# Gated cross-attention with sparse feed-forward on one core: attention in turns of four tiles of scores instead of two, with the loads spread out

## The chip, the cores and the metric

The kernel runs on one core of a Trainium2 chip. The time is the device time of one execution in microseconds (us), median over runs. TensorE (PE in the rows, PEld its weight loads), VectorE (DVE), ScalarE (ACT), GpSimd (POOL) and SyncE (SP, which only issues DMAs here) run in parallel; each works through its own list of instructions in order, and semaphores tie them together.

## The reference

`x` is 32 sequences of 64 tokens with 512 features. Attention has 32 heads of 128 over a context of the same shape, with a bias and a mask of keys; the feed-forward picks one row of 32 in each block by a low-rank score.

```python
x = x + tanh(g_xattn[0]) * xattn(layernorm(x), ctx, mask, bias, Wq, Wk, Wv, Wo)
x = x + tanh(g_ffn[0]) * ffn(layernorm(x), c1, c2, w1, w2t)
# xattn: q, k, v = h @ Wq, c @ Wk, c @ Wv   (32 heads x 128)
#        probs = softmax(q k^T / sqrt(128) + bias, masked); out = (probs v) @ Wo
# ffn:   idx = argmax in each block of 32 of (x @ c1.T @ c2.T)      (1792 = 56 blocks)
#        h = relu(w1[idx] . x);  out = h @ w2t[idx]
```

All of it is float32. The big products are made from high and low parts: three matmuls (hi hi, hi lo, lo hi) in place of one (`three`, L1438 to L1441).

## The kernel before

The kernel has three stages, one behind the other on TensorE.

1. Projections q, k, v of all tokens, in 94 units of seven products each, with results stored to HBM (0 to about 960 us).
2. Attention (about 947 to 1498 us). A *slot* is one tile of 128 tokens (two sequences, a "pair" in the code) with one group of 4 heads. An *iteration* is 8 slots, which share one loaded block of q, k, v (2 MB each), of bias (1 MB) and of Wo. 8 iterations (all head groups) make a half of the tokens; there are 16 iterations and 128 slots. Two slots are a *duo* (DUOS = 64), for which TensorE does: `scores` (q k^T, 64 small matmuls for two duos, L1506), `probs_t` (four transposes of the probabilities, L1522), `attend` (probabilities times values, 64 small matmuls, L1542) and `project_out` (12 long matmuls a slot with Wo, L1439 to L1441). VectorE adds bias and takes the maximum (`scores`, L1137 and L1142), divides (`probs`, L1147 and L1149), takes the low part of the attended values (`clo`, L1227) and adds the projection to `attn_sum` (`add_wo`, L1244; L1242 copies in the first iteration of a half). In the last iteration of each half `add_wo` also applies the gate and adds the residual tile (L1248). ScalarE does the exponentials (`exps`, L863), the copy of the transposed probabilities (`probs_t`, L874) and the high part of the attended values (`chi`, L884). GpSimd adds the mask to the bias (L747) and takes the low parts of weights that are split on the way (L753).
3. Feed-forward (about 1498 us to the end), 16 tiles. Per tile: `selector` (block scores, L1640), `hidden` (inner values, 4 pieces k), transposes of the picked values (`transpose_h`, L1663) and `output`. VectorE finds the winners of the blocks (block_max L1291, is_max L1299, block_first L1304, first_max L1310), picks (`pick_h`, h_picked, L1320) and takes low parts (L1329); GpSimd weighs the ranks (L758). The last turns of attention already hold the start of the first tiles.

The order on every engine is written out by hand, in a loop over duos `d` with special cases at both ends. On TensorE it was: attend both slots of duo d; on every second d the scores of two duos; transposes of duo d+1; projections of both slots of duo d-1. The probabilities have one SBUF buffer `pt`, the transposes banks 3 and 2, the attended values banks 4 and 5, scores 7 and 0, projections 1 and 6.

SyncE issues all loads, in a loop over slots s with p = s mod 8: at p = 2 the next v, at p = 4 and 6 the k and q two iterations ahead, at p = 7 the bias, each behind a wait only for its buffer; pieces of weights (0.5 MB) 3 or 4 slots ahead of their split. "Kept" pieces are the feed-forward's weights: split in attention into high and low part, stored to HBM (`store_kept`) and loaded again later. At the start of attention the second blocks of k and q are loaded by `load_kt(1)` and `load_qt(1)`, behind two pieces of weights.

Of the kernel before, what the change touches and what calls it, by code (L numbers as in the profile page):

```python
# [7 lines left out]
F32 = mybir.dt.float32  # L8
# [48 lines left out]
SCORE_BANK, PT_BANK, PV_BANK, WO_BANK = (7, 0), (3, 2), (4, 5), (1, 6)  # L57
ITERS = HALVES * G
SLOTS = ITERS * PPH
DUOS = SLOTS // 2  # L60
PIECE = 1024
# [13 lines left out]
def pieces():  # L75
# [7 lines left out]
    out.append(("c2", 0, PIECE, SLOTS - 7, "act", "dve"))  # L83
    out.append(("c2", 1, INTER - PIECE, SLOTS - 6, "act", "dve"))
    out.append(("c1", 0, CH * P, SLOTS - 5, "act", "pool"))
# [3 lines left out]
def ffn_uses():  # L89
# [11 lines left out]
    out += [(("sel", 1, k), 2 + k % 2) for k in range(4)]  # L101
    for j in range(PAIRS):
# [19 lines left out]
def build(nc, x, ctx_t, bias, mask, gates, wq, wk, wv, wo, c1, c2, w1, w2, out):  # L122
# [18 lines left out]
    with ExitStack() as whole:  # L141
# [73 lines left out]
        pt = at("probs_t", [P, 2, HG, S], F32, 170)  # L215
# [3 lines left out]
        cxo = [[at(f"attn_t{i}_{n}", [P, 2, HG, P], F32R, (192, 160)[i] + 4 * k) for k, n in enumerate(("hi", "lo"))]  # L219
               for i in range(2)]  # L220

        kept = [at(f"w_{n}_to_keep", [P, PIECE], F32R, 136 + 4 * k) for k, n in enumerate(("hi", "lo"))]
# [12 lines left out]
        x2 = [at(f"x1_tile{i}", [P, D], F32, kb) for i, kb in enumerate((136, 138, 140, 112.5, 157))]  # L235
# [151 lines left out]
        def dest(kind, i):  # L387
# [3 lines left out]
            if kind == "kept":  # L391
                return [t[:, :] for t in kept]
# [38 lines left out]
        def bank_free(use):  # L431
            b = f_before[use]
            if b is None:
                bk = f_bank[use]
                if bk in PT_BANK:
                    return act_pt, DUOS
                return (dve_s, dve_wo, None, None, dve_clo, dve_clo, dve_wo, dve_s)[bk], SLOTS
# [5 lines left out]
        def _(sp):  # L443
# [92 lines left out]
            def store_kept(i):  # L536
                sp.wait_ge(*split_done(piece_no[("kept", i)]))
                for k in range(2):
                    sp.dma_start(kept_d[i, k], kept[k][:, :].bitcast(F32)).then_inc(kept_out, 16)
# [31 lines left out]
            def load_x2(t):  # L571
                if t >= X2R:
                    sp.wait_ge(out_sem[t % X2R], 16 * (t // X2R))
                elif t == 3:
# [63 lines left out]

            for s in range(SLOTS + 5):
                it, p = divmod(s, PPH)  # L640
                if 4 <= s:
                    it4, p4 = divmod(s - 4, PPH)
                    if it4 % G == G - 1 and it4 < ITERS:
                        store_x1(PPH * (it4 // G) + p4)
                for n in range(NP):
# [3 lines left out]
                if s == 0:  # L649
                    load_kt(1)  # L650
                    load_qt(1)
                if s == 1:
                    load_bias(1)
                if p == 2 and it + 1 < ITERS:
                    load_v(it + 1)
                if it + 2 < ITERS:
                    if p == 4:
                        load_kt(it + 2)
                    if p == 6:
                        load_qt(it + 2)  # L660
                    if p == 7:
                        load_bias(it + 2)
                if it % G == G - 1 and it < ITERS:
                    load_x(PPH * (it // G) + p)
                for n in range(NP):
                    if PIECES[n][0] == "kept" and PIECES[n][3] + 2 == s:
                        store_kept(PIECES[n][1])
                if SLOTS - 8 <= s < SLOTS - 8 + W1_PIECES:
                    load_w1(s - SLOTS + 8)
                if s == SLOTS - 14:  # L670
                    sp.wait_ge(kept_out, 32 * KEPT)
                    for t in range(3):
                        load_x2(t)
                if s == SLOTS - 3:
                    load_x2(3)
# [137 lines left out]
        def _(act):  # L813
# [54 lines left out]
            def probs_t(d):  # L868
# [3 lines left out]
                else:  # L872
                    act.wait_ge(pe_pv, 2 * d)
                act.activation(pt[:, :, :, :].rearrange("p a h q -> p (a h q)"),  # L874
                               bank[PT_BANK[d % 2]][:, :], ACT.Copy).then_inc(act_pt, 1)

            def chi(d, h):
                act.wait_ge(pe_pv, 2 * d + 2)
                if d == 0:
# [4 lines left out]
                act.activation(hi, bank[PV_BANK[h]][:, :].rearrange("p (a h q) -> p a h q", a=2, q=S),  # L884
# [78 lines left out]
            for d in range(DUOS + 3):  # L963
                if d == 0:
                    exps(2)
                if d < DUOS:
# [826 lines left out]
```

## Time and profile before

| | us |
|---|---|
| median of 3 runs (1870.86 to 1874.09) | 1872.03 |
| time of the profiled execution | 1874.85 |
| span of its trace, first to last instruction | 1873.0 |
| TensorE busy in it (15304 matmuls) | 1846.8 (99%) |
| VectorE busy | 1070.9 (57%) |
| ScalarE busy | 695.5 (37%) |
| GpSimd busy | 966.2 (52%) |

The granted clock of TensorE, as a mean over the span, is 0.995 of the full 2.4 GHz. The profile is read by stretches, since a share of the whole says nothing about a place; times of rows are microseconds from the start of the span.

### The profile page before, as it was taken

How to read it: one execution, taken by the hardware profiler on the slowest of the kernel's cores; microseconds unless marked ns; L12 is line 12 of the kernel's file. 1: busy time of each engine (PE TensorE's matmuls, PEld its weight loads, DVE VectorE, ACT ScalarE, POOL GpSimd, SP SyncE). 2: the span in 40 equal slices, each digit the busy share in tenths (PEclk: the TensorE clock that was granted, in tenths of full speed). 3: DMA queues.
4: the chain of work that ended last, by engine and by line, in shares of the span. 5: the costliest groups of instructions: out<-in, count | busy, mean ns of one | idle time of the engine just before them, and what ended most of it. 6: DMA issues, size and time to landing. Idle time of an engine off the chain costs nothing.

```text
span 1873.0 us, 37912 instructions
## 1 busy us (share of the span) xinstructions
PE 1846.8 (99%) x15304; PEld 1591.1 (85%) x15304; DVE 1070.9 (57%) x1746; ACT 695.5 (37%) x1773; POOL 966.2 (52%) x766
## 2 busy tenths in 40 slices
PE   8999999999999999999989999999999989999999
PEld 7899988899998888888878888888888778888887
DVE  5333457333345455334356667787667787776763
ACT  4332233322333333333345556555555422222221
POOL 5867688866668888778724334343433121111110
PEclk9999999999999999999999999999999999999999
DMA  5555566644455554467658878798886640000000
GB/s 168 198 176 169 177 200 212 204 158 147 152 181 185 191 186 167 165 223 250 215 225 322 334 281 319 291 387 321 315 321 256 245 181 23 23 28 25 27 12 17
DMA packets 129693, 359.51 MB, mean 192 GB/s; under 512 B 12016, under 2 KB 53360, under 8 KB 118512
## 3 DMA queue, kind: packets, MB, share of 16 engines
q1 hardware_dynamic: 129520, 357.09, 53.2%
q8 instruction: 122, 2.00, 0.5%
q14 instruction: 51, 0.42, 0.1%
HBM read 229.11 MB, written 127.93 MB: 191 GB/s over the span
## 4 chain that ended last, share of the span: by engine, by line
PE 75%; DVE 3%; DMA 1%; issue 1%; ACT 1%; SPq 0%; DVEq 0%
PE bank L1439 21%; PE bank L1441 21%; PE bank L1440 21%; PE bank L1542 3%; PE bank L1506 3%; PE bank L1522 2%; PE bank L1663 1%; PE bank L1640 1%; DVE attn_sum L1248 0%; DMA x_tile<-in_x 0%; DMA x_tile<-x 0%; ACT scores L863 0%; DVE attn_sum L1244 0%; PE bank L1619 0%; DVE attn_t_lo L1227 0%
## 5 line engine op out<-in xcount | busy, mean ns | idle before, releaser
L1439 PE MATMUL bank<-tokens_hi,wkq_hi 128*128 128x512 f32 x888 | 347.6, 391 | 4.8 <-DVE tokens_lo L1043 2.3
L725 POOL TENSOR_TENSOR wkq_lo<-raw_wkq,wkq_hi 128x768 fp32r<-128x768 f32 x126 | 284.1, 2274 | 126.1 <-ACT wkq_hi L827 125.8
L1440 PE MATMUL bank<-tokens_lo,wkq_hi 128*128 128x512 f32 x888 | 346.4, 390 | 0.0
L1441 PE MATMUL bank<-tokens_hi,wkq_lo 128*128 128x512 f32 x888 | 346.2, 390 | 0.0
L1439 PE MATMUL bank<-wv_s_hi,tokens_hi 128*128 128x256 f32 x896 | 254.2, 284 | 0.0
L1441 PE MATMUL bank<-wv_s_hi,tokens_lo 128*128 128x256 f32 x896 | 253.5, 283 | 0.0
L1440 PE MATMUL bank<-wv_s_lo,tokens_hi 128*128 128x256 f32 x896 | 253.5, 283 | 0.0
L1439 PE MATMUL bank<-wo_hi,attn_t_hi 128*128 128x512 f32 x512 | 206.0, 402 | 2.3 <-DVE attn_t_lo L1227 2.3
L1439 PEld LDWEIGHTS bank<-tokens_hi,wkq_hi 128*128 128x128 f32 x888 | 167.2, 188 | 41.1 <-issue 3.8
L1441 PE MATMUL bank<-wo_hi,attn_t_lo 128*128 128x512 f32 x512 | 199.9, 390 | 0.0
L1440 PE MATMUL bank<-wo_lo,attn_t_hi 128*128 128x512 f32 x512 | 199.5, 390 | 0.0
L1441 PEld LDWEIGHTS bank<-tokens_hi,wkq_lo 128*128 128x128 f32 x888 | 167.1, 188 | 35.2
L1440 PEld LDWEIGHTS bank<-tokens_lo,wkq_hi 128*128 128x128 f32 x888 | 167.1, 188 | 33.9
L863 ACT ACTIVATE scores<-scores,negmax 128x64 f32<-128x64 f32 x512 | 172.2, 337 | 48.6 <-DVE negmax L1142 48.6
L725 POOL TENSOR_TENSOR wv_s_lo<-raw_wv,wv_s_hi 128x1536 fp32r<-128x1536 f32 (+1 forms) x32 | 130.1, 4065 | 89.4 <-ACT wv_s_hi L827 89.4
L1065 DVE TENSOR_TENSOR c<-bank,u 128x512 f32<-128x512 f32 x94 | 65.0, 692 | 192.8 <-PE bank L1441 192.8
L852 ACT ACTIVATE p<-bank 128x512 f32<-128x512 f32 x94 | 56.2, 598 | 316.8 <-PE bank L1441 316.8
L1439 PEld LDWEIGHTS bank<-wv_s_hi,tokens_hi 128*128 128x128 f32 x896 | 171.9, 192 | 0.3
L1440 PEld LDWEIGHTS bank<-wv_s_lo,tokens_hi 128*128 128x128 f32 x896 | 172.0, 192 | 0.2
L1441 PEld LDWEIGHTS bank<-wv_s_hi,tokens_lo 128*128 128x128 f32 x896 | 171.9, 192 | 0.0
L753 POOL TENSOR_TENSOR wo_lo<-raw,wo_hi 128x1024 fp32r<-128x1024 f32 x30 | 71.2, 2375 | 169.8 <-DVE wo_hi L1214 169.8
L1087 DVE TENSOR_TENSOR c<-bank,u 128x512 f32<-128x512 f32 x94 | 64.9, 690 | 153.7 <-PE bank L1441 153.4
(146 smaller groups left out, 3706.7 us busy)
## 6 DMA issues: line engine op xcount, KB each, us to landing
k_t<-c SPq DMA_DIRECT2D x128, 256.0 KB, 2.4
v_by_token<-c SPq DMA_DIRECT2D x128, 256.0 KB, 2.3
q_t<-c SPq DMA_DIRECT2D x128, 256.0 KB, 2.3
kt<-k_t SPq DMA_DIRECT2D x16, 2048.0 KB, 9.4
qt<-q_t SPq DMA_DIRECT2D x16, 2048.0 KB, 13.9
v<-v_by_token SPq DMA_DIRECT2D x16, 2048.0 KB, 12.3
raw_wkq<-in_wk SPq DMA_DIRECT2D x32, 512.0 KB, 4.0
raw_wv<-in_wv SPq DMA_DIRECT2D x16, 1024.0 KB, 5.5
```

The lines of the kernel that those rows point to most:

```text
L725: pool.tensor_tensor(lo, job_raw(r)[:, a:b, :], hi.bitcast(F32), ALU.subtract)\
L753: pool.tensor_tensor(lo, raw[n % 2][:, 0:cols], hi.bitcast(F32), ALU.subtract)\
L852: act.activation(e1[n % 2][:, :], bank[n % 2][:, :], ACT.Copy).then_inc(act_e1, 1)
L863: e = act.activation(sc[s % 2][:, h, :], sc[s % 2][:, h, :], ACT.Exp, bias=negmax[s % 2][:, h:h + 1], scale=1.0, accum_out=rsum[s % 2][:, ...
L1065: dve.tensor_tensor(o_c["c12"][n % 2][:, :], bank[5 + n % 2][:, :], u2[:, :], ALU.add)\
L1087: dve.tensor_tensor(o_c["c22"][n % 2][:, :], bank[5 + n % 2][:, :], u3[:, :], ALU.add)\
L1439: pe.matmul(o, a[0], b[0], start=first_mm, stop=False, skip_group_check=not grouped)
L1440: pe.matmul(o, a[0], b[1], start=False, stop=False, skip_group_check=not grouped)
L1441: return pe.matmul(o, a[1], b[0], start=False, stop=last_mm, skip_group_check=not grouped)
L1506: mm = pe.matmul(bank[SCORE_BANK[r % 2]][h * S:(h + 1) * S, o:o + S], qt[it % 2][:, 2 * r_ + h, cols], kt[it % 2][:, 2 * r_ + h, cols], st ...
L1522: mm = pe.transpose(bank[PT_BANK[d % 2]][:, o:o + P], sc[a][:, 2 * r:2 * r + 2, :].rearrange("p h k -> p (h k)"), ident[:, :])
L1542: mm = pe.matmul(bank[PV_BANK[b]][dims, o:o + S], v[it % 2][keys, p, h, dims], pt[keys, s % 2, h, :], start=True, stop=True)
```

## The change

It does the following.

- *Turns.* The loop runs over turns q of two duos a = 2q, b = 2q+1. TensorE: attend a and b; scores of duos b+2 and b+3; projection of slot 2a-2; transposes of duo a+2; projections of slots 2a-1, 2a, 2a+1; transposes of duo b+2. VectorE's and ScalarE's lists are written out to match.
- *Buffers.* `pt` has two buffers. Attended values have two pairs of banks, (3, 5) and (4, 2), and the transposes use the first of each pair. `attend` now waits for `clo` two duos back, and `probs_t` for it too.
- *Loads.* At p = 2 k two iterations ahead; at p = 4, 5 and 7 v, q and bias, each after a wait for a projection (`pe_wo`). `load_kt(1)` and `load_qt(1)` come first of all. The low part of a kept piece is computed in place in the raw buffer, and the load that uses that buffer next waits until the store has landed.
- *Start of attention.* The last product of the projections, `product(93, 3)`, and VectorE's sum of it are moved behind the first `attend`.
- *End.* c1 and c2 are split one slot later; selectors and the low-rank product of tile 0 lie between projections; the inner values of tile 1, pieces 0 and 1, run ahead of tile 0's transposes, with pieces 2 and 3 behind them and other banks for all four.

```diff
-SCORE_BANK, PT_BANK, PV_BANK, WO_BANK = (7, 0), (3, 2), (4, 5), (1, 6)
+SCORE_BANK, PV_BANK, WO_BANK = (7, 0), ((3, 5), (4, 2)), (1, 6)
+PT_BANK = (PV_BANK[0][0], PV_BANK[1][0])
@@ ffn_uses: banks of the inner values
     out += [(("sel", 1, k), 2 + k % 2) for k in range(4)]
+    out += [(("h", 1, k), (2, 3, 0, 1)[k]) for k in range(4)]
...
-            if j + 1 < PAIRS:
+            if 0 < j < PAIRS - 1:
                 out.append((("h", j + 1, k), k % 2))
@@ SyncE
+                    if PIECES[n - 2][0] == "kept":
+                        sp.wait_ge(kept_out, 32 * (PIECES[n - 2][1] + 1))
...
+            load_kt(1)
+            load_qt(1)
...
+                if p == 2 and it + 2 < ITERS:
+                    load_kt(it + 2)
+                if p == 4 and it + 1 < ITERS:
+                    sp.wait_ge(pe_wo, s - 2)
+                    load_v(it + 1)
+                if p == 5 and it + 2 < ITERS:
+                    sp.wait_ge(pe_wo, s - 1)
+                    load_qt(it + 2)
+                if p == 7 and it + 2 < ITERS:
+                    sp.wait_ge(pe_wo, s - 1)
+                    load_bias(it + 2)
...
-                if p == 2 and it + 1 < ITERS:
-                    load_v(it + 1)
-                if it + 2 < ITERS:
-                    if p == 4:
-                        load_kt(it + 2)
-                    if p == 6:
-                        load_qt(it + 2)
@@ VectorE, one turn
+            for q in range(1, TURNS):
+                a, b = 2 * q, 2 * q + 1
+                more = q + 1 < TURNS
+                if more:
+                    scores(2 * a + 4)
+                    scores(2 * a + 5)
+                if q > 1:
+                    add_wo(2 * a - 3)
+                clo(a, 0)
+                if more:
+                    probs(2 * a + 4)
+                clo(a, 1)
+                if more:
+                    probs(2 * a + 5)
...
+                if q > 1:
+                    add_wo(2 * a - 2)
+                splits(a)
+                if more:
+                    scores(2 * b + 4)
+                    scores(2 * b + 5)
+                add_wo(2 * a - 1)
+                if more:
+                    probs(2 * b + 4)
+                clo(b, 0)
+                clo(b, 1)
...
+                add_wo(2 * a)
+                if more:
+                    probs(2 * b + 5)
+                splits(b)
@@ TensorE
+            attend_pair(0)
+            product(NU - 1, 3)
+            project_out(0, heads)
+            probs_t(1)
+            attend_pair(1)
+            scores(3)
+            project_out(1, heads)
+            probs_t(2)
+            project_out(2, heads)
+            scores(4)
+            probs_t(3)
+            for q in range(1, TURNS - 1):
+                a, b = 2 * q, 2 * q + 1
+                attend_pair(a)
+                attend_pair(b)
+                scores(b + 2)
+                if b + 3 < DUOS:
+                    scores(b + 3)
+                project_out(2 * a - 1 if q == 1 else 2 * a - 2, heads)
+                probs_t(a + 2)
+                if q > 1:
+                    project_out(2 * a - 1, heads)
+                project_out(2 * a, heads)
+                project_out(2 * a + 1, heads)
+                probs_t(b + 2)
+            attend_pair(DUOS - 2)
+            attend_pair(DUOS - 1)
+            f_transpose_x(0)
+            f_transpose_x(1)
+            project_out(SLOTS - 6, heads)
+            project_out(SLOTS - 5, heads)
+            low_rank(0)
+            project_out(SLOTS - 4, heads)
+            selector(0, 0)
+            selector(0, 1)
+            project_out(SLOTS - 3, heads)
+            selector(0, 2)
+            selector(0, 3)
...
             hidden(0, 2)
             hidden(0, 3)
+            hidden(1, 0)
+            hidden(1, 1)
             for j in range(PAIRS):
...
+                if j == 0:
+                    hidden(1, 2)
+                    hidden(1, 3)
                 for k in range(4):
-                    if j + 1 < PAIRS:
+                    if 0 < j < PAIRS - 1:
                         hidden(j + 1, k)
                     if j + 2 < PAIRS:
                         selector(j + 2, k)
```

## Rows read from the trace of the kernel before

**Rows 1.** Windows view: window, its length, busy time per engine, clock, DMA share, GB/s.

```profile
961.80:985.50 23.70, 17.67 (x361) 14.86 (x360) 13.87 (x33) 13.12 (x57) 1.92 (x4) 0.88 0.95 368
981.00:984.00 3.00, 2.88 (x54) 2.91 (x56) 0.92 (x2) 0.00 (x0) 0.42 (x1) 0.50 1.03 440
1163.21:1179.52 16.31, 16.31 (x250) 13.63 (x252) 11.25 (x25) 8.90 (x38) 4.83 (x6) 1.00 0.77 287
1228.50:1245.99 17.49, 16.42 (x250) 13.62 (x252) 13.90 (x27) 8.68 (x34) 5.56 (x5) 1.00 1.02 403
1515.00:1523.00 8.00, 5.43 (x22) 4.79 (x23) 5.62 (x10) 0.98 (x2) 3.59 (x1) 0.57 1.03 413
```

**Rows 2.** TensorE timeline, a steady duo: start, duration, line, tiles, count.

```profile
1161.73 0.39 PE L1441 MATMUL bank<-wo_hi,attn_t_lo 128*128 128x512 f32 x1
1162.05 1.16 PE L1542 MATMUL bank<-probs_t,v 64*64 64x64 f32 x64
1163.14 2.08 PE L1506 MATMUL bank<-kt,qt 128*64 128x64 f32 x64
1165.15 0.66 PE L1522 MATMUL bank<-ident,scores 128*128 128x128 f32 x4
1165.56 0.47 PE L1439 MATMUL bank<-wo_hi,attn_t_hi 128*128 128x512 f32 x1
...
1171.20 1.16 PE L1542 MATMUL bank<-probs_t,v 64*64 64x64 f32 x64
```

**Rows 3.** TensorE timeline, transposes behind long matmuls.

```profile
961.57 0.39 PE L1441 MATMUL bank<-tokens_hi,wkq_lo 128*128 128x512 f32 x1
961.80 0.60 PE L1522 MATMUL bank<-ident,scores 128*128 128x128 f32 x4
962.33 1.15 PE L1506 MATMUL bank<-kt,qt 128*64 128x64 f32 x32
...
1535.40 0.60 PE L1663 MATMUL bank<-ident,h_picked 128*128 128x128 f32 x4
1535.75 0.47 PE L1439 MATMUL bank<-w_hi,h_picked_t_hi 128*128 128x512 f32 x1
```

**Rows 4.** TensorE timeline, entry to attention; in brackets idle time and its releaser.

```profile
969.73 0.65 PE L1522 MATMUL bank<-ident,scores 128*128 128x128 f32 x4
971.08 1.16 PE L1542 MATMUL bank<-probs_t,v 64*64 64x64 f32 x64 [0.69 <-ACT probs_t L874]
...
981.12 3.68 PE L1506 MATMUL bank<-kt,qt 128*64 128x64 f32 x64 [2.62 <-issue]
```

**Rows 5.** Groups by line, VectorE, 1010 to 1200: busy, mean ns, idle before.

```profile
L1244 DVE TENSOR_TENSOR attn_sum<-attn_sum,bank 128x512 f32<-128x512 f32 x46 | 31.4, 683 | 8.0 <-PE bank L1441 8.0
```

**Rows 6.** Timelines of VectorE and GpSimd, a gated slot.

```profile
1212.64 2.28 DVE L1248 SCALAR_TENSOR_TENSOR attn_sum<-attn_sum,gate_if_key,x_tile 128x512 f32<-128x512 f32 x1
1212.01 2.36 POOL L753 TENSOR_TENSOR wo_lo<-raw,wo_hi 128x1024 fp32r<-128x1024 f32 x1 [7.80 <-DVE wo_hi L1214]
```

**Rows 7.** DMA issues of 964.3 to 965.9: count, KB, us to landing.

```profile
qt<-q_t SPq DMA_DIRECT2D x1, 2048.0 KB, 16.5
```

**Rows 8.** Timelines of four engines, end of attention and passage to the feed-forward.

```profile
1475.68 0.66 PE L1522 MATMUL bank<-ident,scores 128*128 128x128 f32 x4 [1.28 <-DVE scores L1149]
...
1532.64 0.40 PE L1439 MATMUL bank<-w_hi,h_picked_t_hi 128*128 128x512 f32 x1
...
1516.02 2.02 DVE L1299 TENSOR_TENSOR is_max<-selector,block_max 128x1792 bf16<-128x1792 f32 x1
1527.06 0.69 DVE L1320 SCALAR_TENSOR_TENSOR h_picked<-bank,first_max 128x512 f32<-128x512 f32 x1
...
1518.11 3.59 POOL L758 TENSOR_TENSOR is_max<-is_max,earlier_is_larger 128x1792 bf16<-128x1792 bf16 x1 [15.14 <-DVE is_max L1299]
...
1525.46 0.60 ACT L950 ACTIVATE selector<-bank 128x512 f32<-128x512 f32 x1 [5.66 <-PE bank L1640]
```

More of the change, by code:

```diff
@@ L60 @@
 DUOS = SLOTS // 2
+TURNS = DUOS // 2
 PIECE = 1024
@@ L391, in dest @@
             if kind == "kept":
-                return [t[:, :] for t in kept]
+                return kept[:, :], raw[piece_no[("kept", i)] % 2][:, :].bitcast(F32R)
             if kind == "c1":
@@ L644, in _ @@
                         store_x1(PPH * (it4 // G) + p4)
+                if p == 2 and it + 2 < ITERS:
[9 more added lines that the diff above has]
+                    load_bias(it + 2)
+                for n in range(NP):
+                    if PIECES[n][0] == "kept" and PIECES[n][3] + 2 == s:
+                        store_kept(PIECES[n][1])
                 for n in range(NP):
@@ L1370, in _ @@
                         split(n)
-                if d == DUOS - 6:
+            scores(2)
+            clo(0, 0)
+            clo(0, 1)
+            sum_c12(NU - 1)
+            scores(3)
+            probs(2)
+            probs(3)
+            scores(4)
+            scores(5)
+            add_wo(0)
+            probs(4)
+            clo(1, 0)
+            clo(1, 1)
+            probs(5)
+            splits(0)
+            add_wo(1)
+            scores(6)
+            scores(7)
+            add_wo(2)
@@ L1391, in _ @@
-                if d == DUOS + 1:
-                    block_max(1, 0)
-                    block_max(1, 1)
-                    pick_h(0, 2)
-                    pick_h(0, 3)
-                    block_max(1, 2)
-                    block_max(1, 3)
+            add_wo(SLOTS - 3)
+            f_stats((2, 3))
+            for k in range(4):
+                block_max(0, k)
+            mark_max(0)
+            add_wo(SLOTS - 2)
+            f_norm((2, 3))
+            add_wo(SLOTS - 1)
+            block_rank(0)
@@ L1398, in _ @@
+            first_max(0)
+            pick_h(0, 0)
+            pick_h(0, 1)
+            fx_lo(2)
+            fx_lo(3)
+            block_max(1, 0)
+            block_max(1, 1)
+            pick_h(0, 2)
+            pick_h(0, 3)
+            block_max(1, 2)
+            block_max(1, 3)
             for j in range(PAIRS):
@@ L1541, in attend @@
                         dims = slice(a * S, (a + 1) * S)
-                        mm = pe.matmul(bank[PV_BANK[b]][dims, o:o + S], v[it % 2][keys, p, h, dims],
-                                       pt[keys, s % 2, h, :], start=True, stop=True)
+                        mm = pe.matmul(bank[PV_BANK[s // 2 % 2][b]][dims, o:o + S], v[it % 2][keys, p, h, dims],
+                                       pt[s // 2 % 2][keys, s % 2, h, :], start=True, stop=True)
                 mm.then_inc(pe_pv, 1)
@@ L1610, in _ @@
                 product(n, 4)
-            product(NU - 1, 3)
             probs_t(0)
```

216 lines of the change are left out of this document (87 added, 129 removed).

## The prediction, made before the changed kernel ran

> **What bounds the kernel now.** I read the windows by stage first. In a turn of the middle of attention TensorE is busy 16.31 of 16.31 us, VectorE 11.25, ScalarE 8.90, GpSimd 4.83 [rows 1]. So there TensorE's instruction stream is the time, and a new order can only win what its order itself costs, or lose by new waits. Idle TensorE is found in three other places: the entry to attention (17.67 busy of 23.70 us), the last turns of each half, where VectorE also applies gate and residual (16.42 of 17.49 in the worst), and the passage to the feed-forward part [rows 1]. After the idle stretches at entry and passage the granted clock is at the lower level, 1.2 GHz: 0.50 in 981 to 984, 0.57 on average in 1515 to 1523 [rows 1]. Second view: TensorE's own timeline in each place, for what it waits for and what lies between kinds of matmul. Third: VectorE, GpSimd and the DMA issues in the same stretches.
>
> **Steady turns: a little cheaper.** Before, two pairs of tiles (a "duo") run as probabilities times values, (every second time scores), four transposes, 24 projection matmuls. Two duos take 1.09 + 2.01 + 0.41 + 5.64 [rows 2] and, without scores, 1.10 + 0.41 + 5.65: 16.31. The new turn has the same matmuls: both value products, scores, 12 projections, transposes, 36 projections, transposes. Only neighbours change. A projection that is followed by the value product holds it off 0.32 us (1161.73 to 1162.05, [rows 2]); one that is followed by transposes 0.23 (961.57 to 961.80, [rows 3]). Both of a turn's exits change to that: -0.18. The transposes cost 0.41 each after scores or values [rows 2]; between two runs of long matmuls they cost 0.35, and ahead of a short fp32 kind 0.53 [rows 3]: 0.88 against 0.82, +0.06. Entries into the projections stay two. That is -0.12; since one entry comes from scores, which no row prices, I allow it -0.10 to +0.05 and take -0.11 a turn. The loop has 30 such turns: **-3.3 us** (bounds -6.6 to -2.1 without waits).
>
> Where could TensorE wait in such a turn? (1) The second value product needs ScalarE's copy of the transposes at the end of the turn before. Transposes at 969.73 let the product start at 971.08, 1.35 us later, at the soonest [rows 4]. New: 0.53 + 1.09 = 1.62. Slack 0.27 us, and the ScalarE queue must be free then; it works 8.90 of 16.31. (2) The middle transposes come 1.09 + 1.09 + 2.01 + 2.86 = 7.05 us into the turn, 7.6 after the last ones; VectorE has half of its 11.25 us to do in between, in a chain with ScalarE's exponentials (two sets of 1.4) and copies that I add up to 6.3 from the last transposes on. Slack 1.3. The second half-turn: the same. (3) Value and transpose banks are now shared, so transposes wait for VectorE's low part of the duo two back; that is done 2 us earlier. (4) SyncE now holds the v, q and bias loads until projections are done. The q load goes out 26.7 us into an iteration of 32.6 and is needed at 35.8; alone it should take 7 to 9 us (2 MB), so 0 to 2 us of slack. Behind it on SyncE wait the bias and weight loads, which have 10 us and more. The stored low part is now computed in the raw buffer, so the load of the next piece waits for a store to land; what is queued behind that is the k load, with 20 us in hand. I cost these at nothing; see the rivals.
>
> **Gated turns: dearer.** In the last iteration of a half each add (0.68 us, [rows 5]) is followed by a second operation of 0.75 that reads two SBUF operands. With GpSimd at work it took 2.28: from 1212.64 to 1214.92, while GpSimd's subtraction ran from 1212.01 to 1214.37 [rows 6]. Before, three or four adds were spread so that only 1.07 us was lost in all (mainly a late residual tile) [rows 1]. In the new order three adds fall in the second half-turn (slack 1.3), each 0.86 longer with its link: 2.6 - 1.3 = 1.3 late, and the fourth falls on the subtraction for the piece to keep, 1.5 more in one turn. Two such turns: about 1.3 + 1.5 + 0.3 = 3.1 against 1.07: **+2.0 us** (bounds -1.07, if slack covers all, to +5). On this the Trainium skill, SBUF — State Buffer (section SBUF: two separate sides), says that VectorE and GpSimd take a shared port pair as an exclusive lock, for an instruction of VectorE with two SBUF inputs too. By that rule the collision costs the rest of GpSimd's operation, up to 2.4 us; the trace agrees (2.28). Without it this term would be +0.5.
>
> **Entry to attention.** The last product moves behind the first value product, where TensorE waited for VectorE; the second k and q blocks are now first in the queue and bias, v and the next k come later. Before, the q load issued at 964.54 took 16.5 us [rows 7] and scores(4) waited 2.62 us for it until 981.12 [rows 4]. In the new order it is issued behind the last store, 967.4 by my count: VectorE's last sum runs only after the first low parts, at 966.4. It lands between 979 (4.2 MB at the 440 GB/s of [rows 1], plus 2 us) and 983.9 (again 16.5 us). Before, 1 MB of raw pieces was ahead of it; now it is behind it. I take 981.5. TensorE's way there, from the end of product 4 at 960.4 with the pieces of its own timeline: transposes 960.8 (probabilities ready), scores 961.3, values 962.3, last product 963.4 to 965.0, wait for the low parts to 965.9 (1 us sooner than before, VectorE's sum is out of the way), 12 projections to 968.8, transposes 969.4, 1.35 to the next values 970.8, scores 971.9, projections 972.9 to 975.8, transposes, projections to 979.1. It waits 2.4 there, and has by then done 12 projections (2.86) more and one value product (1.09) less than before: 1.75 ahead, at a moment 0.4 later: **-1.3 us**. The low clock comes again, at the same price. Bounds: +1 (983.9) and -5.8 (979: also the 2.6 us of the low clock stay away).
>
> **End of attention and passage.** Waits of 1.28 [rows 8] and 0.5 us go: the last transposes come 16 us, not a half-turn, after their scores, and selectors stand between projections: -2.0 up to the last hidden product of tile 0. Then half of tile 1's hidden products (24 x 0.227 = 5.4 us) run ahead of tile 0's transposes, where TensorE sat idle 5.8 us. This looks like a gain of 5, but what is late next is VectorE's chain: is_max at 1516.02, GpSimd's rank 1518.11 to 1521.70, two VectorE operations, and h_picked of tile 1 at 1527.06 [rows 8]. The chain hangs on tile 0's first transposes, which are now 5.4 later less 2.0. I get h_picked at 1525.6 to 1526.8. And the diff changes the banks: the selector matmuls of tile 2 now need the banks of hidden products 0 and 1 of tile 1, so selector 1 waits for h_picked 1, which VectorE runs behind block_max 0, which waits for ScalarE's copy of selector 0 (0.49 after its matmul, 0.60 long [rows 8]). Pick 0.7, matmul to copy 0.5, copy 0.6, block_max 0.6, pick 0.7, again 0.5 + 0.6 and the last selector: 4.5 us from h_picked to the first output matmul, so 1530.1 to 1531.3 against 1532.64 [rows 8]: -2.5 to -1.3. But TensorE is then idle some 5 us in 6, longer than before either drop of the clock seen here, so it starts the outputs at 1.2 GHz and loses 1.6 to 3.4 us that were lost before in work that is now waited out. Net **+0.6 us** (bounds -2.5 to +3).
>
> **Sum.** -3.3 + 2.0 - 1.3 + 0.6 = -2.0 us. On the profiled execution (span 1873.0, time 1874.85) that is a span of 1871.0. The median of the runs shown is 1872.03, 2.8 below the profiled time; the same difference from it gives 1870.0 us.
>
> **Rivals.**
> *Loads in ring order.* If the queue serves k and q wholly before what is issued later, q lands at 979 and the clock stays up: 4.5 us more, 1865.5. For it: the k load, issued first, took 5 us less than q. Against: bias and v had moved over 1 MB by q's landing. The Trainium skill, DMA: Bandwidth & Descriptors (section Queues, rings and completion order), has descriptors of one ring consumed in order, which would give this case; the trace bears it out in part. 0.18.
> *The passage pays.* The clock is not lost a second time, or the chain is 2 us shorter: 3 us more, 1867. Against: the bank chain above. 0.14.
> *New wait in each turn.* The copy behind the last transposes is late for the second value product. Decides when ScalarE or the latency adds over 0.27 us; at 0.2 us over in 30 turns that is +6, 1876; at 0.3, 1879. For it: the smallest slack of all. Against: ScalarE is over half idle. 0.15.
> *q lands late.* Over 9 us from issue, in 14 iterations: 0.5 us each is +7, 1877. 0.07. Both are slower than before.
> *It does nothing it says.* Loads collide as before and order is free: 1872. It lies inside the forecast, which has 0.46.
>
> **Chances.** Differences below 0.2% (3.7 us) can't be told from none. Faster by more: the first two rivals, 0.32. Slower: the two wait rivals and part of the gated turns' bound, 0.24. Between: 0.44. The likeliest case alone spans 1868 to 1874. For 8 in 10 I go down to the first rival with 1 us to spare, 1864.5, and up to 1877.5.
>
> **What would show it.** Right: TensorE idle near nothing in middle turns, each 16.2 us long; a wait of 2 to 3 us for q at the first scores(4), then a clock of 0.5; VectorE-caused waits of TensorE at transposes in the last turns of each half; selectors of tile 2 waiting for h_picked, and a clock drop behind 1526. Wrong: turns longer than 16.31, or waits for the probability copy or for q in the middle; no wait at the selectors.

## The result, and the profile after

| | before | after |
|---|---|---|
| median time, us (5 runs each, same chip) | 1872.07 | 1938.29 |
| range, us | 1870.86 to 1874.09 | 1930.1 to 1938.8 |
| span of the profiled execution, us | 1873.0 | 1928.3 |
| TensorE busy in it, us | 1846.8 | 1861.0 |

The ratio is 1.034, interval 1.032 to 1.036. The change makes the kernel 3.4% slower; 0.1% faster was predicted, and the top of the range was 1877.5. The profiled execution is the fastest of the five after (1930.1 us): 55.3 us of the 66 us between the medians stand in its trace, the rest in none.

First view, the windows of after: two middle turns, the first turn with gated adds, the start of attention behind the q load, and the passage.

```profile
1174.36:1190.43 16.07, 16.07 (x250) 13.72 (x249) 10.97 (x25) 8.75 (x38) 4.13 (x6) 1.00 0.74 251
1444.67:1467.42 22.75, 18.72 (x249) 15.80 (x248) 11.23 (x25) 9.60 (x39) 8.46 (x7) 0.85 0.53 193
1222.57:1242.85 20.28, 16.63 (x249) 13.82 (x248) 15.84 (x29) 9.71 (x39) 10.59 (x7) 0.98 1.00 404
982.70:986.10 3.40, 3.40 (x112) 3.07 (x113) 0.61 (x1) 0.60 (x1) 0.00 (x0) 0.50 1.05 447
1583.40:1590.30 6.90, 5.97 (x14) 4.28 (x15) 5.12 (x7) 1.47 (x3) 0.10 (x1) 0.51 0.00 0
```

The first two lines do the same work (250 and 249 matmuls). One takes 16.07 us, less than the 16.31 of before [rows 1]; the other 22.75. VectorE is as busy in it as before (11.23 us), and the DMA share is lower. ScalarE (9.60) and GpSimd (8.46) are busier than in the turn of before in [rows 1], but that isn't the reason: a turn of e1, below, has the same 9.60 and 8.45 and takes 16.07 us. So some middle turns are as good as hoped, and others take up to 6.7 us more. Second view, the four largest of TensorE's waits in the whole span (line, releaser, total, times, longest; L1559 is scores, L1492 a long matmul of the projections, L1573 the transposes of the probabilities, L1691 a selector):

```profile
PE bank L1559 <- issue: 29.0, 13, 4.0
PE bank L1492 <- issue: 5.6, 3, 4.4
PE bank L1573 <- DVE scores L1177: 4.9, 3, 3.6
PE bank L1691 <- DVE h_picked L1346: 3.2, 2, 2.1
```

"Issue" means that the engine waited for nothing that the profile shows. Before, scores had one such wait, that for the q load [rows 4]. Third view, TensorE's timeline at the start of the second window:

```profile
1444.14 0.60 PE L1573 MATMUL bank<-ident,scores 128*128 128x128 f32 x4
1444.67 2.10 PE L1594 MATMUL bank<-probs_t,v 64*64 64x64 f32 x128
1446.69 1.15 PE L1559 MATMUL bank<-kt,qt 128*64 128x64 f32 x31
1451.87 1.44 PE L1559 MATMUL bank<-kt,qt 128*64 128x64 f32 x22 [4.03 <-issue]
```

And the window of the 5 us behind it, where the granted clock is 0.50:

```profile
1452.00:1457.00 5.00, 5.00 (x40) 4.25 (x41) 0.00 (x0) 0.00 (x0) 0.00 (x0) 0.50 0.11 41
```

TensorE stops after 31 of 64 score matmuls. The waits for operands and banks stand ahead of the first and the 33rd of them, not of the 32nd. What can be missing in the middle of such a run is the instructions themselves. The page of the profile has a queue for them. Its first line below is busy time and instructions of each engine, the second that queue (packets, MB, share):

```profile
PE 1861.0 (97%) x15304; PEld 1607.5 (83%) x15304; DVE 1064.3 (55%) x1746; ACT 689.9 (36%) x1773; POOL 966.7 (50%) x766
q8 instruction: 122, 2.00, 0.4%
```

TensorE has 15304 matmuls, as many weight loads, 729 instructions that only wait and two at the ends: 31339 in all. 122 packets of 16 KB make one packet for 257 of them. I numbered TensorE's instructions in the trace in order of their start. Between 985 and 1525 us, 21 gaps between successive starts are longer than 0.5 us. Three have VectorE as their releaser. The other 18, 41.4 us in all, lie at numbers that all leave the remainder 193 when divided by 256. I call these places block boundaries, the 256 instructions between two of them a block, and the gaps there stalls. So TensorE's instructions come in blocks of 256, each in one packet, and in no trace of this study was a boundary in attention crossed earlier than 2.16 us after the start of its packet.

The new turn has one dense run of small matmuls: 128 of attend, 64 of scores, each with its weight load, 384 instructions in 4.04 us (1174.36 to 1178.40). Before, the run was 64 + 64 matmuls, 256 instructions in 3.10 us [rows 2]. A turn is 504 or 505 instructions long, so a boundary lies 7 or 8 instructions deeper in each turn than in the one before. I call the place of the first boundary in a turn its offset. From after's trace, worked out by that numbering (block: time from the boundary before until TensorE goes on behind this one, stall included; delay: from the boundary before to the start of the packet; share: busy share of the data queues in between):

```
turn at   offset  block  delay  share  stall
1000.72    132     7.51   5.14   0.96   4.42   (just behind the dense run)
1174.36    207    10.17   5.59   0.93   0.00   (second boundary of the turn)
1293.81      3     4.02   1.75   0.98   2.00
1402.60     48     6.02   3.65   0.99   3.66
1444.67     63     6.73   4.39   0.92   4.25
1467.42     71     5.97   3.71   0.97   3.43
```

The stall is the delay plus 2.2 to 2.5 us, less what the block would have taken by itself (2.5 us for an offset of 63). A long delay makes a long stall, but a block that TensorE uses up fast stalls with a short one too (1293.81: delay 1.75, stall 2.00). SyncE's timeline for the same two turns (from 1444.67 and from 1467.42):

```profile
1444.33 0.32 SPq L524 DMA_DIRECT2D v<-v_by_token  x1
1445.94 0.33 SPq L537 DMA_DIRECT2D raw<-in_w  x1
...
1467.08 0.33 SPq L519 DMA_DIRECT2D bias_in<-in_bias  x1
1467.46 0.43 SPq L537 DMA_DIRECT2D raw<-in_wo  x1
1467.94 0.43 SPq L541 DMA_DIRECT2D w_hi_lo<-w_hi_to_keep  x1
1468.41 0.66 SPq L542 DMA_DIRECT2D w_hi_lo<-raw  x1
```

v waits for `pe_wo` s-2 and bias for s-1. Both are the last projection ahead of a dense run. The change gives out 2.5 MB, in two or in four transfers, within 1.3 us of the start of the dense run, here and in most other turns.

The 55.3 us between the spans: the stalls at boundaries are 41.4 us. Behind the long ones TensorE runs at its lower clock, 1.2 GHz. After's busy time is 18.1 us above that of the same work with few stalls (1842.9 in e1, below). The two make 59.5; the rest is small and of both signs.

### The profile page after: what moved, and what is told of

Read it like the earlier page. It is cut to its first block, busy times and chain, and to the rows that moved or that the text cites. A ratio compares the mean times of both kernels' runs of the same rounds, so it can differ in the third digit from the quotient of the medians.

```text
span 1928.3 us, 37953 instructions
## 1 busy us (share of the span) xinstructions
PE 1861.0 (97%) x15304; PEld 1607.5 (83%) x15304; DVE 1064.3 (55%) x1746; ACT 689.9 (36%) x1773; POOL 966.7 (50%) x766
## 4 chain that ended last, share of the span: by engine, by line
PE 74%; issue 2%; DMA 2%; DVE 2%; ACT 0%; SPq 0%; POOL 0%; DVEq 0%; ACTq 0%
PE bank L1492 21%; PE bank L1494 21%; PE bank L1493 21%; PE bank L1559 3%; PE bank L1594 3%; PE bank L1573 1%; PE bank L1714 1%; DMA bias_in<-in_bias 1%; DMA x_tile<-in_x 1%; PE bank L1691 1%; PE bank L1670 0%; DMA x_tile<-x 0%; DVE scores L1177 0%; DVE is_max L1325 0%; ACT scores L870 0%
## 5 line engine op out<-in xcount | busy, mean ns | idle before, releaser
L1492 PE MATMUL bank<-tokens_hi,wkq_hi 128*128 128x512 f32 x888 | 347.8, 392 | 5.9 <-DVE tokens_lo L1071 2.6
L1492 PE MATMUL bank<-wv_s_hi,tokens_hi 128*128 128x256 f32 x896 | 254.2, 284 | 0.0
L1492 PE MATMUL bank<-wo_hi,attn_t_hi 128*128 128x512 f32 x512 | 210.7, 411 | 5.4 <-issue 4.7
L1492 PEld LDWEIGHTS bank<-tokens_hi,wkq_hi 128*128 128x128 f32 x888 | 167.1, 188 | 42.2 <-issue 4.0
L1492 PEld LDWEIGHTS bank<-wv_s_hi,tokens_hi 128*128 128x128 f32 x896 | 171.9, 192 | 0.3
```

Of the source, the lines that this page charges most:

```text
L1492: pe.matmul(o, a[0], b[0], start=first_mm, stop=False, skip_group_check=not grouped)
```

## Experiments

The pieces of the theory: F, TensorE's instructions arrive late (F1: because data is moving; F2: by a fixed time of its own); L, the held-back loads arrive late; W, a late step of VectorE or ScalarE. Times are medians; "1.0017 [1.0008, 1.0025]" is the ratio to the kernel before on the same chip with its interval. The kernel before took 1872.6 to 1874.2 us beside them.

**The offset of the blocks alone (e1, e2).**

```diff
+            def step():
+                pe.wait_ge(pool_c, 1)
+                pe.wait_ge(pool_c, 2)
@@ product: one step() in each of the first 174 (e1) or 57 (e2) products from unit 30 on
@@ project_out: ahead of heads 1 to 3, until 7 or 8 are used in a turn
+                    if h and in_turn[0]:
+                        in_turn[0] -= 1
+                        step()
```

> The changed kernel with instructions that do nothing (waits long met) added to TensorE's list: 174 of them in the projections of stage 1, and 7 or 8 in each turn, so that a turn is 512 instructions long and not 504 or 505. Nothing else is touched. Theory F (TensorE's instruction stream comes in blocks of 256 instructions, and the dense run of 384 small-matmul instructions in the new turn uses one up before the next has landed): with this offset a block boundary lies in the middle of the dense run (214 instructions into a turn) in every turn, as in the turns at 1127 to 1245 us of the changed kernel, which do not stall. So no stalls, turns of 16.1 us, 1867 to 1874 us. Theory L (loads held back or arriving late) and theory W (a late VectorE or ScalarE step): nothing of theirs changes, 1936 to 1942 us.

Measured: 1876.93 us, 1.0017 [1.0008, 1.0025].

> As the run before it, but with 57 of the empty instructions ahead of attention: a block boundary then lies 75 instructions into each turn and the next one 331 in, so that one whole block is used up in the dense run in each of 29 turns. Theory F: every turn stalls as the worst of the changed kernel do (3 to 4 us and more, some at the low clock): 1970 to 2030 us. Theories L and W: 1936 to 1942 us, the same as with the other offset.

Measured: 2020.65 us, 1.0778 [1.0753, 1.0804]. The two kernels differ only in how many empty instructions run ahead of attention, and are 144 us apart. The waits view, e1 (its scores are L1568), then e2:

```profile
PE bank L1568 <- issue: 1.9, 1, 1.9
...
PE bank L1568 <- issue: 95.0, 30, 4.1
```

In e1 the one such wait left at scores is for the q load; 25 of its 28 middle turns take 16.07 to 16.10 us, such as:

```profile
1145.47:1161.54 16.07, 16.07 (x249) 13.73 (x248) 11.32 (x25) 9.60 (x39) 8.45 (x7) 1.00 0.90 356
```

F holds, and L and W can't explain a single one of these 144 us. e1 landed 3 us above F's range; where, is said below.

**The loads as before (e3).** Undo the order and the `pe_wo` waits of the loads of k, v, q and bias.

> The changed kernel with SyncE's loads of k, v, q and bias in attention where the kernel before has them (k at p = 4, v at 2, q at 6) and without the waits for projections. Theory L: the time that was lost comes back, 1870 to 1880 us. Theory F: TensorE's list is not touched, the stalls stay in the same turns: 1930 to 1945 us. Theory W: 1936 to 1942.

Measured: 1896.81 us, 1.0121 [1.0107, 1.0134]. Neither theory said that: TensorE's list is that of after, and still two thirds of the loss is gone. The stalls still lie at remainder 193 only, but they are 12 and not 18, and 18.2 us in sum, not 41.4. So how late the blocks are depends on where the loads stand: F1, with L's edit as its second half.

**The dense run cut in two (e4).**

```diff
                 attend_pair(a)
-                attend_pair(b)
                 scores(b + 2)
+                project_out(2 * a - 1 if q == 1 else 2 * a - 2, heads)
+                attend_pair(b)
                 if b + 3 < DUOS:
                     scores(b + 3)
-                project_out(2 * a - 1 if q == 1 else 2 * a - 2, heads)
```

> The changed kernel with TensorE's dense run cut in two: attend a, scores b+2, 12 projection matmuls, attend b, scores b+3. Same number of instructions, same offsets of the blocks. Theory F: a block now takes at least some 5 us to use up, no stalls; one more change of kind of matmul in each turn costs up to 0.3 us x 30: 1868 to 1880 us. Theory L: 1936 to 1942. Theory W: attend b comes 2.9 us later, so VectorE's chain is tighter, not slower than 1936 in any case.

Measured: 1915.80 us, 1.0223 [1.0199, 1.0248]. A miss. A turn without stalls now takes 16.51 us, 0.44 more for the two changes of kind; TensorE waits 15.1 us in 14 places for VectorE's probabilities; and 14.9 us of stalls are left, since a block takes 5.4 us there and the delays go up to 5.8 us, after which the 2.2 us still come. Cutting the run helps only as far as the delay is short. A block that lasts over 5 us is not safe by that alone: the longest stall here is 2.6 us.

**Less data at the same moments (e5).**

> The kernel of e2_phase_bad (2020.65 us) with less data to load: from the third iteration on the loads of k, q and v move only a quarter of their block (one head of four, two tiles of eight), so its attention works in part on old data. TensorE's list and the semaphores are the same. In e2 the stalling block's packet starts 3 to 4.4 us after TensorE entered the block before, with the data queues over 0.9 busy, and TensorE goes on 2.2 to 2.5 us after the packet's start; where the queues were idle (share below 0.3) packets started from 1.8 us before to 1.1 us after. Theory F1 (the fetch waits behind data in the DMA engines): with most of the traffic gone the stalls shrink from 3.3 us to 0 to 0.8 us in most turns: 1875 to 1905 us. Theory F2 (the fetch's own time is fixed, data traffic has no part in it): 2010 to 2030 us.

Measured: 1989.08 us, 1.0613 [1.0591, 1.0634]. A miss for both theories: over the 30 short blocks (under 8 us) the stalls fell from 3.3 us in e2 to 2.8 on average, not to 0.8. The loads are smaller, but they still start with the dense run, and packets of 4 KB instead of 16 KB moved at 230 to 280 GB/s, so that data was under way for 4 us nonetheless. Two blocks met quiet queues (share below 0.35, and 0.00): delays 0.39 and 0.67 us, stalls 0.70 and 0.12.

**The same amount of data, later (e9, e10).**

```diff
                 if p == 4 and it + 1 < ITERS:
-                    sp.wait_ge(pe_wo, s - 2)
+                    sp.wait_ge(pe_wo, s - 1)
                     load_v(it + 1)
@@ p == 7
-                    sp.wait_ge(pe_wo, s - 1)
+                    sp.wait_ge(pe_wo, s)
                     load_bias(it + 2)
```

> The kernel of e2_phase_bad (2020.65 us) with two of SyncE's waits moved by one projection: v's load waits for one projection more, and so does the bias load. In the changed kernel the projection that they wait for is the last one ahead of the dense run, so v (2 MB), or bias (1 MB), a piece of Wo and two stores, are issued within 0.4 us of the start of every dense run (1444.33 for a run from 1444.67, 1467.08 to 1468.41 for one from 1467.42). In e5_bad_light less volume was loaded, but still at that moment, and it still stalled 2 to 4 us. Theory F1 (the fetch of a block waits when data starts to move at that moment): the stalls shrink from 3.3 us to at most 1.5, 1900 to 1950 us. Theory F2 (data has no part in it): 2010 to 2030 us.

Measured: 1957.83 us, 1.0449 [1.0433, 1.0465]. At the worst offset, TensorE's waits at scores and at attend (L1603) are now these (e2's row is above), and the first 3 to 5 us of a dense run look like this, e2 first, then e9:

```profile
PE bank L1568 <- issue: 25.0, 25, 3.2
PE bank L1603 <- ACT probs_t L881: 19.7, 13, 1.7
```

```profile
1443.10:1448.00 4.90, 2.99 (x157) 2.78 (x149) 4.16 (x11) 4.07 (x19) 2.15 (x3) 1.00 0.96 348
```

```profile
1443.10:1446.00 2.90, 2.90 (x153) 2.73 (x145) 2.23 (x6) 2.48 (x11) 2.90 (x3) 1.00 0.39 102
```

Same instructions, same offset; 348 GB/s against 102. In e2 the packet of the next block starts 4.43 us after the boundary and TensorE is busy 2.99 of 4.90 us; in e9 it starts 0.57 us after it and TensorE does not stop (0.24 us). Over all short blocks (under 8 us): with a share above 0.85 the delay was 2.9 to 4.5 us in e2 (28 blocks) and 2.3 to 3.8 in e9 (15 blocks); with a share below 0.35 it was 0.4 to 1.1 us in e9 (14 blocks) and the stall 0.2 to 0.9. Where the blocks stand, the data makes the delay: F1 is shown, F2 is out. The time is 8 us above F1's range all the same. In 12 of the 15 other blocks the stall is gone (0.0 to 0.2 us) for another reason: TensorE waits inside the block, which then lasts 5.7 to 6.9 us. It waits for the copy of the probabilities (19.7 us in 13 places, from this edit, as the next run shows) and ahead of the 33rd score matmul, where it needs the next q (1.1 us at 1465.79); the row of issue waits above holds both kinds, boundaries and operands that land late.

> The changed kernel with those two waits moved by one projection and nothing else; no empty instructions. F1: most of the 64 us come back, as far as no other load starts at a dense run: 1878 to 1900 us. F2: 1930 to 1945 us.

Measured: 1949.06 us, 1.0419 [1.0390, 1.0447], 11 us slower than after. A miss in the other direction. The boundary stalls went down to 15.6 us, as F1 has it, but my own edit brought waits:

```profile
PE bank L1594 <- ACT probs_t L881: 19.7, 13, 1.7
PE bank L1559 <- issue: 15.3, 15, 2.0
PE bank L1573 <- DVE scores L1177: 12.9, 5, 5.0
PE bank L1594 <- issue: 10.3, 10, 1.9
```

Behind v in SyncE's list stands a piece of weights. It lands too late for ScalarE, which splits it ahead of the copy of the probabilities (ScalarE's timeline):

```profile
1495.97 1.06 ACT L941 ACTIVATE w_hi_to_keep<-raw 128x1024 fp32r<-128x1024 f32 x1 [5.07 <-DMA raw<-in_w]
1496.93 0.58 ACT L881 ACTIVATE probs_t<-bank 128x512 f32<-128x512 f32 x1
```

**The kernel before at its worst offset (e6).** 200 empty instructions ahead of attention, 7 or 8 in every two duos.

> The kernel before with 200 empty instructions ahead of attention and 7 or 8 in every two duos, so that a block boundary lies 4 instructions into each run of attend and scores (256 instructions, some 3.1 us), and the next at its end, in every second duo. Theory F: the shorter dense run gives the fetch 3.1 us, against 2.6 in the changed kernel at its worst; with packets that start 1 to 4 us late in the busy stretches it stalls 0.5 to 1.5 us in about half of the 29 places: 1880 to 1905 us. If the kernel before is safe whatever its offset (only the run of 384 matters): 1872 to 1876 us, which also is the price of the empty instructions.

Measured: 1882.35 us, 1.0044 [1.0027, 1.0060]. The kernel before can stall too. Its blocks take 3.1 us there; where the delay is above 0.8 us it loses 0.1 to 0.7, once 3.15 us, and 3.1 us more at the entry. So even at its worst offset it loses 9 us where the changed kernel loses 144 against e1. That its run is shorter and its loads don't start with it fits this; the two were not tried apart. At its own offset no boundary of its attention costs it more than 0.3 us.

**Other parts, with the blocks out of the way (e7, e8).** e7 takes e1 and puts the four hidden products of tile 1 and their banks back; e8 takes e1 and puts the loads back as in e3.

> The kernel of e1_phase_mid (1876.93 us) with the passage to the feed-forward part as before: the four hidden products of tile 1 behind the transposes of tile 0, on the banks of before. By the prediction's step (the new order costs 0.6 us) 1876.3 us. By the trace of e1 (selectors wait 1.39, 2.06 and 0.32 us, TensorE at 1.2 GHz behind them, 1.8 us more from the first output matmul to the end than before) the new order costs 2 to 4 us: 1873 to 1875 us.

Measured: 1876.65 us, 1.0017 [1.0008, 1.0026], 0.3 below e1. From the last turn to the end e7's trace takes 401.1 us and e1's 403.6, one execution each; the time does not show this difference (e1's runs spread over 5 us, e7's over 3). Between 0.3 us by the medians and 2.5 by the two traces the price of the new passage stays open.

> The kernel of e1_phase_mid with the loads of k, v, q and bias in attention as before and without the waits for projections. Only with the block boundaries out of the dense run can this part be priced alone. Prediction's step: the loads are in time either way, so 1876 to 1878 us, no difference. Theory L (the later loads cost something of their own, by q landing late): 1 to 4 us less than e1.

Measured: 1876.99 us, 1.0023 [1.0013, 1.0034]. No difference from e1. By themselves the later loads cost nothing.

The pair says one thing more. TensorE's list and the offset are the same in e1 and e8, and in the long block of a turn the data queues are busy with a share of 0.95 and more in both (e8: 27 of 28). Yet the delay is 3.1 to 5.5 us in 26 of 28 such blocks of e1, and 2.1 to 2.7 in 22 of 28 of e8 (0.7 to 4.0 in the others). So a busy queue alone doesn't set the delay; it also depends on which loads were given out, and when. By what rule, no run here shows.

**The gated turns, and the start of attention (e11 to e14).** In e11, e12, e13 and e14 the third add of a gated turn stands behind the last probs:

```diff
+                last = a // 4 % G == G - 1
+                if not last:
+                    add_wo(2 * a)
-                add_wo(2 * a)
                 if more:
                     probs(2 * b + 5)
+                if last:
+                    add_wo(2 * a)
```

> The kernel of e1_phase_mid (1876.93 us) with the two waits moved, the loads of the residual tiles ahead of the other loads of their slot, and in the gated turns the third add_wo of a turn behind the last probs (which TensorE's transposes wait for: 4.35 us at 1229.81 in e1). If the gated turns are late because probs stands behind an add that waits for its residual tile: 3 to 5 us less than e1, 1872 to 1874 us. If the rest of VectorE's chain is late anyway: 1875 to 1877 us.

Measured: 1958.91 us, 1.0464 [1.0442, 1.0486]. A miss: the moved waits of e10 again. At e1's offset there is one wait more, for v itself (attend, TensorE's timeline; v was issued at 1298.51, and loads of v took up to 16.8 us to land in this trace):

```profile
1312.31 1.99 PE L1607 MATMUL bank<-probs_t,v 64*64 64x64 f32 x64 [4.74 <-issue]
```

> The kernel of e1_phase_mid (1876.93 us) with SyncE's waits left as in the changed kernel, only the gated add moved behind the last probs in the two gated turns of each half, and with 210 instead of 174 empty instructions ahead of attention: a block boundary then lies 178 instructions into each turn, so that both blocks of a turn last about 8 us (10.1 and 5.95 in e1), and the stall of 3.5 us at the start of attention and the one of 1.5 in the last turn should shrink. If the wait of 4.35 us in the gated turns comes from probs behind an add that waits for its residual tile, it goes down to 1 to 2: 1868 to 1873 us, level with the kernel before or up to 0.3% faster. If the shared port or the chain behind it is what is late: 1873 to 1876 us.

Measured: 1885.76 us, 1.0062 [1.0048, 1.0076]. The wait for probs in the gated turns is gone, but an offset of 178 is worse than 214. I had balanced the two blocks of a turn at 8 us each. With 214 the block that begins in the dense run lasts 10.1 us, and the packet behind it mostly starts 0.7 to 1.8 us before the boundary is even crossed. With 178 a delay of 5.3 to 6.0 us ends too late in eight turns (1.0 to 1.6 us each).

> The kernel of e1_phase_mid (1876.93 us), offset and all, with only the third add_wo of a gated turn moved behind the last probs. In e12_gated_only the wait of 4.35 us for probs was gone, but its offset brought stalls of 1.0 to 1.6 us in nine turns. If the prediction's gated turns were under-costed and this is their place: 4 to 5 us less than e1, 1871.5 to 1873 us. If the time only moves to another wait in the same turns: 1875 to 1877 us.

Measured: 1877.78 us, 1.0019 [1.0010, 1.0028], e1's time. The time moved on. e1 first, the place that was mended (TensorE, VectorE); then e13, VectorE:

```profile
1229.81 0.66 PE L1582 MATMUL bank<-ident,scores 128*128 128x128 f32 x4 [4.35 <-DVE scores L1177]
```

```profile
1226.52 0.75 DVE L1274 SCALAR_TENSOR_TENSOR attn_sum<-attn_sum,gate_if_key,x_tile 128x512 f32<-128x512 f32 x1 [1.52 <-DMA x_tile<-in_x]
1227.19 0.17 DVE L1175 RECIPROCAL rowinv<-rowsum 128x4 f32<-128x4 f32 x1
1227.40 2.36 DVE L1177 TENSOR_TENSOR scores<-scores,rowinv 128x256 f32<-128x256 f32 x1
```

```profile
1233.88 0.75 DVE L1274 SCALAR_TENSOR_TENSOR attn_sum<-attn_sum,gate_if_key,x_tile 128x512 f32<-128x512 f32 x1 [3.83 <-DMA x_tile<-in_x]
```

The next gated add waits 3.83 us for its residual tile, and TensorE waits 2.94 us for the q of the next half (issued at 1220.51, 12.7 us to landing); the two gated turns take 16.07 and 22.94 us, where e1 had 20.63 and 17.63.

> The kernel of e13_mid_gated with the 174 empty instructions moved from stage 1 into the projections of the first turn, 14 or 15 ahead of each head, so that the first turns keep the offset of the changed kernel (block boundary 99 instructions into the first dense run, stall there 0.5 to 1.6 us against 3.5 in e1) and all later ones that of e1. If an empty instruction costs TensorE nothing in the projections even in such numbers: 2 to 3 us less than e13, 1869 to 1871 us. If each holds it up by some 30 ns: 3 to 5 us more than that.

Measured: 1885.12 us, 1.0065 [1.0051, 1.0079]. A miss: packed 14 to 15 in a row, the empty instructions cost time. The first turn takes 28.13 us against 18.31 in e13, which has a stall 2.2 us longer there: by an estimate from these two traces (9.8 + 2.2) / 174 = 69 ns each. Spread as 7 or 8 over a turn they cost nothing (16.07 us with and without). No version of the new order came out below the kernel before.

## Why the prediction was wrong

**Steady turns: the step that failed is the list of places where TensorE could wait.** It named four, all of them semaphores, and the sum took a turn for right if its operands are there. The supply of instructions was not on it, so its cost stood at nothing in the sum; it measured 41.4 us of stalls and some 18 us of lower clock in one execution. The trace of before had what pointed at it: the packet count of the instruction queue, and the run of small matmuls that grows from 256 instructions in 3.1 us to 384 in 4.0. The size could not be read from it, since its boundaries in attention cost 0.3 us at most. The order of work was weighed as matmul neighbours only. The Trainium skill, Runtime: NRT & Kernel Launch (section Instruction fetch mechanics), says that instructions come in blocks of 256 which the engine fetches ahead while it executes. The trace agrees (31339 / 122 = 257). It also says that crossing a block is mostly hidden. In the kernel before it is; here the measurement decides, with up to 4.4 us at one boundary and 41.4 us in all.

**Steady turns, size without stalls.** Predicted 16.20 us; 16.07 to 16.08 measured. The sign was right and the term too small: two value products in a row take 2.02 us (1174.36 to 1176.38), not twice 1.09. Over 30 turns that is -7, not -3.3.

**Waits in the turn.** Held: the copy of the probabilities, 0.27 us of slack, is waited for in no middle turn of after or e1 (one wait of 0.7 us in each, at the entry as before). It became the wait that was feared only in e9 to e11 (13 to 15 times, up to 3.9 us); the row of e10 shows a late piece of weights ahead of it in ScalarE's list. q costs nothing in the middle turns (e8).

**The loads.** They were read for their latest landing alone. That a load's start can hurt, because the wait ties it to the start of a dense run, was not asked. With this edit and the offset, one effect needs both: e1 removes 61 us by the offset, e3 41 us by the loads.

**Gated turns: 3.1 us predicted, 5.4 found** (1222.57 to 1242.85 is 4.2 over a plain turn, the next 1.2; 6.1 in e1). The long VectorE operation is there: 2.36 us for probs at 1227.40 in e1, against 0.43 otherwise, beside a subtraction of GpSimd from 1227.08 to 1229.47, as in [rows 6]. What was missing is the residual tile that lands late (1.5 us in e1, 3.8 in e13), and the lower clock after the idle time: e1's second gated turn takes 17.63 us without a wait, at a mean clock of 0.90.

**Entry: right up to scores(4).** Predicted 981.5 after 2.4 us of waiting, measured 981.34 after 2.29, and then the clock of 0.50 (rows above). q landed there and not 2.5 us sooner, so the rival by the Trainium skill's rule of rings served in order (DMA: Bandwidth & Descriptors, section Queues, rings and completion order) did not come about. What followed was not in the sum: a boundary stall of 1.6 us in after and 3.2 to 3.5 in e1, e12 and e13. The bound of -5.8 was 0.5 us short of its own terms (1.3, the 2.4 of waiting and the 2.6 of the low clock); nothing hung on it.

**Passage: right in mechanism.** The selectors of tile 2 wait for h_picked and the clock drops behind them, 0.51 in 1583.40 to 1590.30. From h_picked (1580.70) to the first output matmul (1585.93) 5.2 us, predicted 4.5. The price, 0.6 by the prediction, is between 0.3 and 2.5 (e7).

**Rivals.** All of them dealt with semaphores and data. The nearest, a new wait in each turn, had the right shape (a small loss 30 times) and the wrong resource, and its price of 0.2 to 0.3 us a turn was a tenth of what was found. In e1, where the blocks are out of the way, the prediction can be judged as it stood: +2.7 us against -2.0, with 5.0 us of boundary stalls left in it, at the entry and in the last turn. Without them it would be about -2.3. That the sum is so close is luck, two errors that cancel: the turns were worth 3.8 us more, the gated turns cost 3 us more.

## What to carry to other kernels

Ask of a long run of small matmuls how many instructions it has, weight loads counted, and how long 256 of them last. In these traces a block stalled when it lasted less than the delay plus 2.2 to 2.5 us. The blocks of 2.0 to 2.6 us in the dense run stalled nearly every time while data was moving; but blocks of 5.4 us (e4) and of 6.7 us (e12) stalled too, by up to 2.6 and 1.6 us, where the delay had grown to 5 or 6 us. The sign in a profile is an "issue" wait in the middle of a group that waits for nothing, at places a multiple of 256 instructions apart. And a load given out by an event of TensorE starts at that event in every turn: look at what TensorE does in the 5 us behind it.

## What the runs showed of the hardware

- A block's packet itself takes 0.9 to 1.5 us (once 2.3, in e6), and behind a stall TensorE goes on 2.2 to 2.9 us after its start (minimum 2.16; in after 2.2 to 2.5). What varies is when it starts: 0.4 to 1.1 us behind the boundary before with quiet data queues (e2, e5, e9). With busy ones it is mostly 3 to 6 us where the loads are given out with the dense run (after, e1, e2), up to 8.5 at the start of attention (e12), but with the same share 0.6 to 2.1 in seven short blocks of after (from the turn at 1276.19 to that at 1386), 0.4 to 1.5 in most short blocks of e6 and 2.1 to 2.7 in most long ones of e8.
- In projections the packet can start 1 to 3 us before the boundary is crossed. So nearly the same 256 instructions were harmless with the boundary 12 instructions ahead of the dense run (after, turn at 1260.12: no stall) and not with 4 ahead (turn at 1276.19: 1.43 us).
- A number of instructions that do nothing moved the time of this kernel by 7.7%.
